# Two images' patches per block of partitions in the tokenizer's last layer and norm

## The chip, the cores and the metric

The kernel runs on one core of a Trainium2 chip. The metric is the device time of one launch in microseconds, from the core's first instruction to its last with what the launch itself adds. Engines are named as in the profile: PE (TensorE, matmuls), DVE (VectorE), ACT (ScalarE), POOL (GpSimd), SP (here only a queue that issues DMAs).

## The reference, cut to what matters

A tokenizer turns 32 images into 49 patch tokens of 192 features each, ends in a depthwise and a pointwise convolution and a layer norm over the features, and is followed by a state space block (Mamba) and an attention and mixture-of-experts block. Only the end of the tokenizer and how it meets the Mamba block matter here.

```
h = relu(dwconv(h, f1_dw, f1_pw, f1_pwb))
h = relu(dwconv(h, f2_dw, f2_pw, f2_pwb))
h = dwconv(loc + h, f3_dw, f3_pw, f3_pwb)          # [B, 192, 7, 7]
t = transpose(h.reshape(B, 192, 49), (0, 2, 1))     # [B, 49, 192]
mu = mean(t, -1); var = mean((t - mu) ** 2, -1)
t = (t - mu) / sqrt(var + 1e-05) * ln_g + ln_b
h = concatenate([cls, t, txt], axis=1)              # [B, 82, 192]
h = h + mamba(layernorm(h)); h = h + attention_and_experts(layernorm(h))
```

## The kernel before

The 32 images run in four chunks `c` of eight (`CH = 4`, `IM = 8`) through a pipeline of seven waves `w`. In wave `w`, chunk `w` is in the first convolutions, and the three fusion layers `f1`, `f2`, `f3` (index `k` = 0, 1, 2) work on chunks `w-1`, `w-2`, `w-3`. A depthwise layer has 192 channels in two tiles of 96 partitions: DVE does tile 0 with nine instructions of 441 elements that add up in PSUM (`dw`, lines 176 and 178), and ACT and POOL do tile 1 (nine products, `weigh`, L346; eight sums, `add_up`, L494). PE then does the pointwise layer. For `f1` and `f2` the result has channels in partitions (L239). For `f3` PE takes the image as the stationary operand, so that patches come out in partitions: each image gives 49 partitions x 192 (L302). Two images fill one PSUM bank, a *fill*; three banks rotate, so fill `n` waits until DVE has taken fill `n - 3`.

DVE takes a fill with the bias added (`take_rows`, L416) into `T0`, 49 partitions x 32 images x 192, computes mean and variance of each image's 49 rows (L422, L425), POOL computes the reciprocal root (`roots`, L481, L483, ready as `s_rs`), and `norm_rows` ends the norm: one instruction per image for `(t - mean) * root` (L431), then two over the whole chunk for `* ln_g` (L434) and `+ ln_b` (L436). SP stores each finished chunk into `H` (tokens in partitions) with one DMA (L206).

The order on each engine is the order in which the code is written. In wave `w` DVE runs `norm_rows(w-5)` and `take_rows(w-4)` ahead of the depthwise work of `f2` and `f3`; after the last wave it runs `take_rows(3)`, `norm_rows(2)`, `norm_rows(3)`. The Mamba block's first round is woven in through `tail(...)` points: `z` (L1182) from PE matmuls (L866, L869) and ACT (L1008 to L1047), which need the stored chunk 0; `R` (L1187) behind PE's L891; a zeroing of PSUM (L1271); then the statistics of the stored chunks 1 to 3 (`chunk_stats`, L1166 to L1173), the step size (L1190 to L1200), and the scan, whose inputs POOL makes (L1356) and which DVE runs (L1238).

Of the kernel before, what the change touches and what calls it, by code (L numbers as in the profile page):

```python
# [95 lines left out]
def tokenizer(nc, ctx, at, ps, H, vec, ident, eye, xcol, w_pl, w_pg, had, pw_mix, w96, vecs, pwb_row, lng_row, lnb_row, cls_row, txt):  # L96


    if True:
# [27 lines left out]
        T0 = P1[0:PATCHES].rearrange("p k n -> p (k n)")[:, 0:B * D].rearrange("p (b c) -> p b c", b=B)  # L127
        rows = sb("rows", [PATCHES, 3, D])
        st = sb("st", [PATCHES, IM, 6])
        mv = sb("mv", [PATCHES, B, 2])  # L130
        ve = sb("ve", [PATCHES, B])
        rs = sb("rs", [PATCHES, B])
        nh = sb("nh", [PATCHES, B])
# [3 lines left out]
        f3_bank = [psC[0:PATCHES, 0, 0:2 * D], psC[0:PATCHES, 1, 0:2 * D], psC[0:PATCHES, 2, 0:2 * D]]  # L137
# [52 lines left out]
        def sync(sp, tail):  # L190
# [13 lines left out]
            for c in range(CH):  # L204
                sp.wait_ge(s_t1, c + 1)
                sp.dma_start(H[1:1 + PATCHES, c * IM:(c + 1) * IM, :], T0[:, c * IM:(c + 1) * IM, :]).then_inc(s_out[c], 16)  # L206
                if c == 1:
                    sp.wait_ge(s_lr, CH)
                    tail("last sums")

        def tensor(pe, tail):
# [32 lines left out]
            for w in range(WAVES):  # L244
# [46 lines left out]
                if 0 <= w - 3 < CH:  # L291
# [5 lines left out]
                    for n in range(c * IM // 2, (c + 1) * IM // 2):  # L297
                        if n >= 3:
                            pe.wait_ge(s_t0, n - 2)
                        for j in range(2):  # L300
                            for k in range(2):
                                mm = pe.matmul(f3_bank[n % 3][:, j * D:(j + 1) * D], dense(DF[2], k)[:, 2 * n + j - c * IM, :],  # L302
                                               wf[:, 3, k, :], start=k == 0, stop=k == 1)
                        mm.then_inc(s_f[2], 1)

        def scalar(act, tail):
# [2161 lines left out]
```

## Time and profile before

| | |
|---|---|
| median of 3 runs | 1454.99 us (1440.70, 1454.99, 1455.33) |
| the profiled execution | 1444.48 us |
| its span, first to last instruction | 1442.7 us, 1.78 us less than its time |
| granted TensorE clock, mean over the span | 0.92 of full speed |
| busy share of the span | PE 85%, PEld 54%, DVE 72%, ACT 49%, POOL 54% |
| end of the tokenizer (first input of the scan starts on POOL) | 301.46 us after the start |

The busy shares are means over stages of different kinds. The change lies in the last 110 us of the first 301 us; what happens behind 301 us is the same program in both kernels, and starts when the step `dtz` of L1200 is done. A granted clock of 0.50 is the lower of TensorE's two levels (1.2 GHz), 1.00 the upper (2.4 GHz).

### The profile page before, as it was taken

How to read it: one execution, taken by the hardware profiler on the slowest of the kernel's cores; microseconds unless marked ns; L12 is line 12 of the kernel's file. 1: busy time of each engine (PE TensorE's matmuls, PEld its weight loads, DVE VectorE, ACT ScalarE, POOL GpSimd, SP SyncE). 2: the span in 40 equal slices, each digit the busy share in tenths (PEclk: the TensorE clock that was granted, in tenths of full speed). 3: DMA queues.
4: the chain of work that ended last, by engine and by line, in shares of the span. 5: the costliest groups of instructions: out<-in, count | busy, mean ns of one | idle time of the engine just before them, and what ended most of it. 6: DMA issues, size and time to landing. Idle time of an engine off the chain costs nothing.

```text
span 1442.7 us, 19486 instructions
## 1 busy us (share of the span) xinstructions
PE 1220.1 (85%) x5820; PEld 783.0 (54%) x5821; DVE 1043.2 (72%) x1983; ACT 705.7 (49%) x1490; POOL 778.8 (54%) x499
## 2 busy tenths in 40 slices
PE   6895845547889899999986789999999799999996
PEld 4342322223445445454543457887777567777775
DVE  3699778798989999999999745677778653333332
ACT  1137732167677686867675235545543232222221
POOL 3027975197787968788787420134445465222222
PEclk9797656779999999999999989999999599999998
DMA  5200000044042240404050001112222123222221
GB/s 171 57 1 0 29 9 29 17 162 141 12 130 70 72 140 0 140 0 140 11 160 1 0 5 57 42 47 72 56 64 65 36 54 54 38 37 35 37 36 20
DMA packets 71201, 81.00 MB, mean 56 GB/s; under 512 B 13230, under 2 KB 62917, under 8 KB 71129
## 3 DMA queue, kind: packets, MB, share of 16 engines
q1 hardware_dynamic: 51986, 69.29, 15.4%
q0 software_dynamic: 17152, 9.24, 4.7%
q10 hardware_dynamic: 1992, 1.59, 0.4%
q8 instruction: 37, 0.61, 0.2%
q14 instruction: 34, 0.28, 0.1%
HBM read 48.74 MB, written 30.01 MB: 55 GB/s over the span
## 4 chain that ended last, share of the span: by engine, by line
PE 55%; DVE 20%; ACT 9%; issue 8%; POOL 5%; DMA 2%; DVEq 0%; SPq 0%; POOLq 0%; ACTq 0%
PE ps L2131 10%; PE ps L955 6%; PE ps L2150 6%; DVE hs L1238 5%; PE ps L1610 3%; PE ps L866 3%; PE ps L1553 3%; POOL DF L494 2%; PE ps L239 2%; PE ps L2140 2%; PE ps L1623 2%; ACT ps L1108 2%; DVE ps L178 2%; PE ps L932 2%; PE ps L232 2%
## 5 line engine op out<-in xcount | busy, mean ns | idle before, releaser
L1356 POOL TENSOR_TENSOR Bx<-dtz,Bb 128x984 f32<-128x984 f32 x128 | 289.4, 2283 | 41.2 <-DVE hs L1238 27.3
L1238 DVE TENSOR_TENSOR_SCAN hs<-ps,Bx 128x492 f32<-128x492 f32 x256 | 287.6, 1164 | 22.2 <-POOL Bx L1356 12.8
L1108 ACT ACTIVATE ps<-dt,A 128x324 f32<-128x324 f32 (+1 forms) x512 | 211.5, 456 | 79.5 <-DVE hs L1238 76.5
L955 PE MATMUL ps<-hs,b_id 128*128 128x492 f32 x512 | 235.9, 583 | 12.0 <-DVE y L1205 9.3
L2250 POOL DMA_INDIRECT out<-yt,dest x48 | 74.7, 1557 | 166.4 <-DVE yt L2236 160.2
L1248 DVE TENSOR_TENSOR hs<-hs,ps 128x984 f32<-128x984 f32 x128 | 150.2, 1173 | 1.9
L2131 PE MATMUL ps<-W,xT 97*128 (+1 forms) x384 | 143.1, 516 | 3.8 <-ACT hb L2188 1.4
L955 PEld LDWEIGHTS ps<-hs,b_id 128*128 128x128 f32 x512 | 92.2, 193 | 79.1 <-issue 73.8
L2220 DVE COPY hT__5873<-ps 128x768 f32<-128x768 f32 x48 | 46.0, 958 | 115.8 <-PE ps L2140 113.6
L1999 POOL DMA_INDIRECT buckets<-XS,c_slot x64 | 90.9, 1420 | 38.2 <-issue 25.0
L2150 PE MATMUL ps<-W,hT__5873 128*128 x576 | 109.2, 327 | 0.8 <-DVE yb L2230 0.8
L2188 ACT ACTIVATE hb<-ps 128x768 f32<-128x768 f32 x48 | 39.0, 812 | 143.4 <-PE ps L2131 143.4
L2006 POOL TENSOR_TENSOR c_x<-c_x,bro 82x192 f32<-82x192 f32 x32 | 19.2, 600 | 161.7 <-DVE c_x L1795 161.6
L2131 PEld LDWEIGHTS ps<-W,xT 97*128 97x128 f32 (+1 forms) x384 | 71.8, 197 | 58.1 <-issue 21.6
L2150 PEld LDWEIGHTS ps<-W,hT__5873 128*128 128x128 f32 x576 | 91.4, 190 | 1.4 <-issue 1.4
L494 POOL TENSOR_TENSOR DF<-DF,prod 96x441 f32<-96x441 f32 x84 | 87.4, 1041 | 6.6
L940 PE MATMUL ps<-P,sel 96*128 96x328 bf16 x128 | 40.2, 315 | 52.8 <-DVE hs L1248 40.4
L1756 DVE TENSOR_REDUCE mx<-ps 82x12 f32<-82x984 f32 x32 | 37.6, 1176 | 60.4 <-PE ps L1610 60.4
L1623 PEld LDWEIGHTS ps<-V,PT 82*82 82x82 f32 x768 | 64.6, 160 | 10.8 <-issue 4.3
L940 PEld LDWEIGHTS ps<-P,sel 96*128 96x128 bf16 x128 | 12.3, 97 | 100.5 <-DVE hs L1248 65.9
L1623 PE MATMUL ps<-V,PT 82*82 82x17 f32 x768 | 63.1, 228 | 1.7 <-DVE XN L1788 1.7
L1610 PE MATMUL ps<-kB,qT 128*82 128x328 f32 (+1 forms) x256 | 61.9, 386 | 3.1 <-DVE E L1760 2.0
(273 smaller groups left out, 2424.4 us busy)
## 6 DMA issues: line engine op xcount, KB each, us to landing
Bb<-b_rows SPq DMA_DIRECT2D x32, 656.0 KB, 7.4
buckets<-b_zero SPq DMA_DIRECT2D x8, 2288.0 KB, 15.3
xg<-buckets SPq DMA_DIRECT2D x48, 104.0 KB, 2.0
xc<-in_xcol SPq DMA_DIRECT2D x4, 1176.0 KB, 9.3
W<-in_w1d SPq DMA_DIRECT2D x8, 582.0 KB
W<-in_w2d SPq DMA_DIRECT2D x8, 576.0 KB
out<-H SPq DMA_DIRECT2D x8, 246.0 KB
H<-P SPq DMA_DIRECT2D x4, 294.0 KB
```

The source lines that it names most:

```text
L494: g.tensor_tensor(out, a, prod[:, (9 * n + t) % PRODUCTS], ALU.add).then_inc(s_sum, 1)
L955: mm = pe.matmul(ps[:, BANK_Y + h, 0:HALF], ident[:], f2(hs[:, s % LONG])[:, h * HALF:(h + 1) * HALF], start=s == 0, stop=s == STATE - 1)
L1108: a = act.activation(ps[:, BANK_A + h, c:c + w].rearrange("p (g t) -> p g t", t=S)[:, :, 1:S], dt[:, (par + t // STATE) % 2, m, g0 * S:g1 ...
L1238: v.tensor_tensor_scan(f2(hs[:, t % LONG])[:, c], ps[:, BANK_A + h, 0:HALF], f2(Bx[:, t % RING])[:, c], 0.0, ALU.mult, ALU.add).then_inc(s ...
L1248: v.tensor_tensor(hs[:, s % LONG], hs[:, s % LONG], ps[:, BANK_C + s % 2, 0:N].rearrange("p (a n) -> p a n", a=1).broadcast_to([128, NI, N ...
L1356: g.tensor_tensor(Bx[:, t % RING], dtz[:, p], Bb[:, p, t % STATE, :].rearrange("p (a n) -> p a n", a=1).broadcast_to([128, NI, N]), ALU.mu ...
L1610: mm = pe.matmul(ps[0:S, SCORES + h0 // 6, (h0 % 6) * S:(h0 % 6 + h1 - h0) * S], qT[:, par, m_, q * S:(q + 1) * S], kB[:, par, m_, q, j:j ...
L1623: mm = pe.matmul(ps[0:S, HEAD_OUT + c % 2, h * (DH + 1):(h + 1) * (DH + 1)], PT[:, c % 2, h, :], V[:, vpar, c, h, :], start=True, stop=True)
L1999: g.indirect_dma_start(out=xs, out_offset=bass.IndirectOffsetOnAxis(ap=slot[:, p % 2, k, c:c + 1], axis=0), in_=slots(p)[:, c, :], in_offs ...
L2131: mm = pe.matmul(ps[:, UP + h, 0:384], xT[c_, p, k, :], W1[c_, k, bass.ds(e, 1), h * 384:(h + 1) * 384].rearrange("p a n -> p (a n)"), sta ...
L2150: mm = pe.matmul(ps[:, Y, 0:D], hT[:, p, k, :], W2[:, k, bass.ds(e, 1), :].rearrange("p a n -> p (a n)"), start=k == 0, stop=k == KF - 1)
L2250: g.indirect_dma_start(out=out, out_offset=bass.IndirectOffsetOnAxis(ap=dest[:, p:p + 1], axis=0), in_=yt[:, p, :], in_offset=None, comput ...
```

## The change

- The stationary operand of `f3` becomes two images at once. Images lie 56 columns apart in `DF` (eight rows of seven, the eighth row is padding), so 56 + 49 = 105 columns hold two images, and PE writes 105 partitions: image `2i` in partitions 0 to 48, image `2i+1` in 56 to 104, unused rows between. A chunk has four such pairs and two fills instead of eight images and four fills.
- `T0`, the rows of bias, scale and shift, and the statistics are laid out for 105 partitions and half as many blocks.
- `take_rows` now also does `(t - mean) * ln_g` in one fused instruction per pair; it needs no root. `norm_rows` is one fused instruction per pair, `t * root + ln_b`. Both have two tensor inputs in SBUF.
- `norm_rows(2)` moves ahead of `take_rows(3)`.
- Each chunk is stored by two DMAs of 49 partitions x 4 images x 192 instead of one of 49 x 1536.

```diff
+        TWO, PAIRS = ROW * GRID + PATCHES, IM // 2
+        T0 = P1[0:TWO].rearrange("p k n -> p (k n)")[:, 0:CH * PAIRS * D].rearrange("p (b c) -> p b c", b=CH * PAIRS)
...
-                sp.dma_start(H[1:1 + PATCHES, c * IM:(c + 1) * IM, :], T0[:, c * IM:(c + 1) * IM, :]).then_inc(s_out[c], 16)
+                images = H[1:1 + PATCHES, c * IM:(c + 1) * IM, :].rearrange("p (n h) d -> p h n d", h=2)
+                for h in range(2):
+                    sp.dma_start(images[:, h], T0[h * ROW * GRID:h * ROW * GRID + PATCHES, c * PAIRS:(c + 1) * PAIRS, :]).then_inc(s_out[c], 16)
...
-                    for n in range(c * IM // 2, (c + 1) * IM // 2):
+                    for n in range(c * FILLS, (c + 1) * FILLS):
                         if n >= 3:
                             pe.wait_ge(s_t0, n - 2)
                         for j in range(2):
+                            b = 4 * n + 2 * j - c * IM
                             for k in range(2):
-                                mm = pe.matmul(f3_bank[n % 3][:, j * D:(j + 1) * D], dense(DF[2], k)[:, 2 * n + j - c * IM, :],
+                                both = DF[2][:, k].rearrange("p r c -> p (r c)")[:, b * ROW * GRID:b * ROW * GRID + TWO]
+                                mm = pe.matmul(f3_bank[n % 3][:, j * D:(j + 1) * D], both,
                                                wf[:, 3, k, :], start=k == 0, stop=k == 1)
...
-                v.wait_ge(s_t0, (c + 1) * IM // 2)
-                for b in range(c * IM, (c + 1) * IM):
-                    i = own.did(v.bn_stats(st[:, b % IM, :], T0[:, b, :]))
+                v.wait_ge(s_t0, (c + 1) * FILLS)
+                for b in range(c * PAIRS, (c + 1) * PAIRS):
+                    i = own.did(v.bn_stats(st[:, b % PAIRS, :], T0[:, b, :]))
                 own.need(i)
-                for b in range(c * IM, (c + 1) * IM):
-                    v.bn_aggr(mv[:, b, :], st[:, b % IM, :]).then_inc(s_mv, 1)
+                for b in range(c * PAIRS, (c + 1) * PAIRS):
+                    v.bn_aggr(mv[:, b, :], st[:, b % PAIRS, :]).then_inc(s_mv, 1)
+                v.wait_ge(s_mv, (c + 1) * PAIRS)
+                for b in range(c * PAIRS, (c + 1) * PAIRS):
+                    i = own.did(v.scalar_tensor_tensor(T0[:, b, :], T0[:, b, :], mv[:, b, 0:1], rows[:, 1, :], ALU.subtract, ALU.mult))
+                own.need(i)
 
             def norm_rows(c):
 
                 v.wait_ge(s_rs, c + 1)
-                for b in range(c * IM, (c + 1) * IM):
-                    i = own.did(v.tensor_scalar(T0[:, b, :], T0[:, b, :], mv[:, b, 0:1], rs[:, b:b + 1], ALU.subtract, ALU.mult))
-                own.need(i)
-                t = T0[:, c * IM:(c + 1) * IM, :]
-                i = own.did(v.tensor_tensor(t, t, rows[:, 1:2, :].broadcast_to([PATCHES, IM, D]), ALU.mult))
-                own.need(i)
-                v.tensor_tensor(t, t, rows[:, 2:3, :].broadcast_to([PATCHES, IM, D]), ALU.add).then_inc(s_t1, 1)
+                for b in range(c * PAIRS, (c + 1) * PAIRS):
+                    i = v.scalar_tensor_tensor(T0[:, b, :], T0[:, b, :], rs[:, b:b + 1], rows[:, 2, :], ALU.mult, ALU.add)
+                i.then_inc(s_t1, 1)
...
+            norm_rows(CH - 2)
             take_rows(CH - 1)
-            norm_rows(CH - 2)
             tail("last rows")
             norm_rows(CH - 1)
```

On DVE in wave 5, from the norm of chunk 0 to the start of `f2`'s depthwise work of chunk 3, there stood before (`P_58` is `T0`, `mv` holds mean and variance, `rs` the root, `rows` bias, scale and shift):

```order
L431 TENSOR_SCALAR P_58<-P_58,mv,rs 49x192 x8
L434 TENSOR_TENSOR P_58<-P_58,rows 49x1536
L436 TENSOR_TENSOR P_58<-P_58,rows 49x1536
L416 TENSOR_TENSOR P_58<-ps,rows 49x384 x4
L422 BN_STATS st<-P_58 49x6 x8
L425 BN_AGGR mv<-st 49x2 x8
L176 TENSOR_SCALAR ps<-PF_60,vec 96x441
```

and now:

```order
L441 SCALAR_TENSOR_TENSOR P_58<-P_58,rs,rows 105x192 x4
L422 TENSOR_TENSOR P_58<-ps,rows 105x384 x2
L428 BN_STATS st<-P_58 105x6 x4
L431 BN_AGGR mv<-st 105x2 x4
L434 SCALAR_TENSOR_TENSOR P_58<-P_58,mv,rows 105x192 x4
L178 TENSOR_SCALAR ps<-PF_60,vec 96x441
```

The norm of chunk 0 is four instructions instead of ten, and four of another kind stand behind the statistics of chunk 1; the same two rows repeat in the other waves.

On DVE behind the last depthwise work (`DF_65` is its result) there stood before:

```order
L178 SCALAR_TENSOR_TENSOR DF_65<-PF_61,vec,ps 96x441
L416 TENSOR_TENSOR P_58<-ps,rows 49x384 x4
L422 BN_STATS st<-P_58 49x6 x8
L425 BN_AGGR mv<-st 49x2 x8
L431 TENSOR_SCALAR P_58<-P_58,mv,rs 49x192 x8
L434 TENSOR_TENSOR P_58<-P_58,rows 49x1536
L436 TENSOR_TENSOR P_58<-P_58,rows 49x1536
L1271 MEMSET ps 128x1024
L1182 SCALAR_TENSOR_TENSOR z<-sg,ps 128x328
```

and now:

```order
L180 SCALAR_TENSOR_TENSOR DF_65<-PF_61,vec,ps 96x441
L441 SCALAR_TENSOR_TENSOR P_58<-P_58,rs,rows 105x192 x4
L422 TENSOR_TENSOR P_58<-ps,rows 105x384 x2
L428 BN_STATS st<-P_58 105x6 x4
L431 BN_AGGR mv<-st 105x2 x4
L434 SCALAR_TENSOR_TENSOR P_58<-P_58,mv,rows 105x192 x4
L1277 MEMSET ps 128x1024
L1188 SCALAR_TENSOR_TENSOR z<-sg,ps 128x328
```

The norm of chunk 2 now stands ahead of the taking of chunk 3's fills, where DVE waits for PE.

On PE at the join of the two blocks, from the fills of chunk 2 over the Mamba block's first transposes (L860) and projections there stood before:

```order
L239 MATMUL ps<-DF_64,wf 96x392 x4
L302 MATMUL ps<-wf,DF_65 49x192 x16
L860 MATMUL ps<-b_id,hn 128x82 x8
L866 MATMUL ps<-hT,wzg 128x328 x2
L869 MATMUL ps<-hT,wzg 128x328 x2
```

and now:

```order
L243 MATMUL ps<-DF_64,wf 96x392 x4
L308 MATMUL ps<-wf,DF_65 105x192 x8
L866 MATMUL ps<-b_id,hn 128x82 x8
L872 MATMUL ps<-hT,wzg 128x328 x2
L875 MATMUL ps<-hT,wzg 128x328 x2
```

Eight matmuls of the same length replace sixteen (each stands as two records in the trace).

## Rows read from the trace of the kernel before

**Rows 1.** The chain that ended last, 190 to 262 us: start, length (us), what.

```profile
195.28 1.69 POOL rs L483
196.99 9.51 DVE P L431 x8
206.53 2.66 DVE P L434
...
211.48 2.81 PE ps L302 x8
...
235.95 8.42 PE ps L302 x32
...
259.36 8.67 PE ps L302 x32
```

**Rows 2.** Timeline of DVE: start, us, engine, line, operation, count, [idle before, releaser].

```profile
214.90 2.17 DVE L422 BATCH_NORM_STATS2 st<-P 49x6 f32<-49x192 f32 x8
217.10 0.63 DVE L425 BATCH_NORM_AGGREGATE mv<-st 49x2 f32<-49x6 f32 x8
...
235.99 2.40 DVE L431 TENSOR_SCALAR P<-P,mv,rs 49x192 f32<-49x192 f32 x8 [0.16 <-DVE DF L178]
...
240.21 1.75 DVE L436 TENSOR_TENSOR P<-P,rows 49x1536 f32<-49x1536 f32 x1
...
249.28 0.50 DVE L1182 SCALAR_TENSOR_TENSOR z<-sg,ps 128x328 f32<-128x328 f32 x1 [4.33 <-ACT sg L1047]
...
252.47 0.50 DVE L1182 SCALAR_TENSOR_TENSOR z<-sg,ps 128x328 f32<-128x328 f32 x1
...
268.05 0.55 DVE L416 TENSOR_TENSOR P<-ps,rows 49x384 f32<-49x384 f32 x1 [0.75 <-PE ps L302]
...
277.53 0.91 DVE L1271 MEMSET ps<- 128x1024 f32 x1 [0.21 <-issue]
278.36 0.47 DVE L1182 SCALAR_TENSOR_TENSOR z<-sg,ps 128x328 f32<-128x328 f32 x1
...
284.64 0.48 DVE L1187 TENSOR_TENSOR R<-ps,P 64x328 f32<-64x328 f32 x1
...
291.85 2.17 DVE L1166 BATCH_NORM_STATS2 b_st<-H 82x6 f32<-82x192 f32 x8
...
299.65 1.67 DVE L1200 TENSOR_TENSOR dtz<-dt,z 128x984 f32<-128x984 f32 x1
```

**Rows 3.** Timeline of POOL.

```profile
196.94 1.98 POOL L520 TENSOR_TENSOR PF<-L,R 96x392 f32<-96x392 f32 x2
...
199.94 7.62 POOL L494 TENSOR_TENSOR DF<-DF,prod 96x441 f32<-96x441 f32 x7
...
253.55 1.66 POOL L483 TENSOR_TENSOR rs<-ve,nh 49x8 f32<-49x8 f32 x1
```

**Rows 4.** Groups of DVE by form: busy us, mean ns of one.

```profile
L1205 DVE SCALAR_TENSOR_TENSOR y<-z,vec,ps 128x164 f32<-128x164 f32 x16 | 5.4, 376 | 0.0
```

**Rows 5.** Timeline of ACT.

```profile
237.25 5.08 ACT L346 ACTIVATE prod<-PF,vec 96x441 f32<-96x441 f32 x9
244.84 0.54 ACT L1008 ACTIVATE hT<-ps,vec 128x328 f32<-128x328 f32 x1 [2.52 <-PE ps L860]
```

**Rows 6.** Timeline of PE.

```profile
246.62 1.34 PE L866 MATMUL ps<-hT,wzg 128*128 128x328 f32 x4 [1.53 <-ACT hT L1011]
247.89 0.82 PE L869 MATMUL ps<-hT,wzg 64*128 64x328 f32 x4
...
278.98 5.54 PE L891 MATMUL ps<-z,wx 128*96 128x328 f32 x12 [8.92 <-DVE z L1182]
```

**Rows 7.** Windows: stretch, length, busy us (count) of PE, PEld, DVE, ACT, POOL, granted clock, DMA share, GB/s.

```profile
50.00:54.00 4.00, 3.40 (x5) 1.03 (x6) 0.39 (x1) 0.00 (x0) 0.00 (x0) 0.62 1.09 277
240.00:242.00 2.00, 2.00 (x8) 1.25 (x7) 1.97 (x3) 2.00 (x5) 0.00 (x0) 0.50 0.00 0
242.00:244.00 2.00, 2.00 (x13) 1.51 (x12) 1.44 (x3) 0.32 (x1) 0.00 (x0) 0.97 0.20 52
```

More of the change, by code:

```diff
@@ L125, in tokenizer @@
         R2 = sb("R2", [HD, 2, NP])
[L127 to L133, printed above, removed]
+        TWO, PAIRS = ROW * GRID + PATCHES, IM // 2
+        T0 = P1[0:TWO].rearrange("p k n -> p (k n)")[:, 0:CH * PAIRS * D].rearrange("p (b c) -> p b c", b=CH * PAIRS)
+        rows = sb("rows", [TWO, 3, D])
+        st = sb("st", [TWO, PAIRS, 6])
+        mv = sb("mv", [TWO, CH * PAIRS, 2])
+        ve = sb("ve", [TWO, CH * PAIRS])
+        rs = sb("rs", [TWO, CH * PAIRS])
+        nh = sb("nh", [TWO, CH * PAIRS])
         psC, psF, psA, psB = ps[:, 0:3, :], ps[:, 3, :], ps[:, 4:6, :], ps[:, 6:8, :]
-        f3_bank = [psC[0:PATCHES, 0, 0:2 * D], psC[0:PATCHES, 1, 0:2 * D], psC[0:PATCHES, 2, 0:2 * D]]
+        f3_bank = [psC[0:TWO, 0, 0:2 * D], psC[0:TWO, 1, 0:2 * D], psC[0:TWO, 2, 0:2 * D]]
+        FILLS = PAIRS // 2
         s_wp = sem("a_wp"); s_small = sem("a_small"); s_wc = sem("a_wc"); s_x = [sem("a_x0"), sem("a_x1")]
@@ L311, in scalar @@
             for k, row in enumerate((pwb_row, lng_row, lnb_row)):
-                act.dma_start(rows[:, k, :], row.rearrange("(a c) -> a c", a=1).broadcast_to([PATCHES, D])).then_inc(s_rows, 16)
+                act.dma_start(rows[:, k, :], row.rearrange("(a c) -> a c", a=1).broadcast_to([TWO, D])).then_inc(s_rows, 16)
             act.wait_ge(s_small, 64)
@@ L412, in take_rows @@
             def take_rows(c):
-                for n in range(c * IM // 2, (c + 1) * IM // 2):
+                for n in range(c * FILLS, (c + 1) * FILLS):
                     v.wait_ge(s_f[2], n + 1)
                     v.tensor_tensor(T0[:, 2 * n:2 * n + 2, :], f3_bank[n % 3].rearrange("p (j c) -> p j c", j=2),
-                                    rows[:, 0:1, :].broadcast_to([PATCHES, 2, D]), ALU.add).then_inc(s_t0, 1)
+                                    rows[:, 0:1, :].broadcast_to([TWO, 2, D]), ALU.add).then_inc(s_t0, 1)
@@ L477, in roots @@
             def roots(c):
-                g.wait_ge(s_mv, (c + 1) * IM)
-                a = slice(c * IM, (c + 1) * IM)
+                g.wait_ge(s_mv, (c + 1) * PAIRS)
+                a = slice(c * PAIRS, (c + 1) * PAIRS)
                 n = own.did(g.tensor_scalar(ve[:, a], mv[:, a, 1], 1e-5, None, ALU.add))
@@ L505, in gpsimd @@
                         if w - k - 1 > 0:
[L506 removed]
+                            g.wait_ge(s_f[k], (w - k - 1) * (FILLS if k == 2 else 1))
                         add_up(k, w)
@@ L820, in _ @@
                 if j == 0:
-                    sp.wait_ge(tok.s_out[CH - 1], 16)
+                    sp.wait_ge(tok.s_out[CH - 1], 32)
                     sp.dma_start(wug[:], w_ug).then_inc(s_wug, 16)
@@ L943, in first @@
             def first():
-                pe.wait_ge(tok.s_t0, CH * IM // 2)
+                pe.wait_ge(tok.s_t0, CH * IM // 4)
                 pe.sem_inc(s_left, 1)
@@ L1163, in chunk_stats @@
                 a = slice(c * IM, (c + 1) * IM)
-                v.wait_ge(tok.s_out[c], 16)
+                v.wait_ge(tok.s_out[c], 32)
                 for b in range(c * IM, (c + 1) * IM):
@@ L1269, in tail @@
                 if point == "last rows":
-                    v.wait_ge(tok.s_t0, CH * IM // 2)
+                    v.wait_ge(tok.s_t0, CH * IM // 4)
                     v.memset(ps[:, BANK_A:BANK_A + 2, :], 0.0).then_inc(s_cst, 1)
```

3 lines of the change are left out of this document (1 added, 2 removed).

## Prediction

> **What bounds the kernel now.** I read the chain of waits first, from 190 to 302 us. From 195.28 us it runs over POOL's root, then DVE's norm of chunk 0, PE's fills and DVE's depthwise work, down to `dtz`, whose end starts the scan [rows 1, 2]. So DVE sets the end of the tokenizer, with PE in between twice: the fills of chunk 2 and of chunk 3, 8.42 and 8.67 us, each of which DVE needs whole before it goes on [rows 1]. Ahead of 195 us POOL's sums set the pace, and DVE waits for their root; what is saved on DVE there is worth nothing. Behind 301 us both kernels run the same program, begun by one event, so an earlier `dtz` shifts all of it. The second view is the timeline of POOL beside DVE's. The same eight norm instructions (L431) cost 9.51 us beside POOL's additions and 2.40 us when POOL is idle [rows 1, 2]; 1.98 us for POOL's pair L520 and seven times its pitch of 7.62 / 7 = 1.09 us make 9.6 [rows 3]. Each of them gets one gap between two POOL instructions. The addition of 1536 elements shows the same: 2.66 us with POOL at work, 1.75 us without [rows 1, 2]. Third, the granted clock: it is at the lower level when a group of fills begins and rose at about 242 us, six microseconds into the fills of chunk 2; in the two windows PE did 8 and then 13 matmul records in 2 us [rows 7].
>
> **The price of the new instruction.** No instruction of the trace adds two SBUF tensors with a scalar read per partition. The nearest (L1205, 164 elements, one input in PSUM) took 376 ns [rows 4]; with 28 elements more it is about 400 ns, or 0.37 us from start to start, so four cost 1.5 us when POOL is idle. Beside POOL's chain the bounds are those 0.37 us (no conflict) and 1.98 us each (each waits for a pair like L520). I take 1.09 us, the pitch at which L431 went, since the addition with two SBUF inputs was held up in the same way.
>
> The Trainium skill (SBUF — State Buffer, Who interferes with whom) says that DVE and GpSimd share a pair of ports by an exclusive lock, and that a DVE instruction with two SBUF inputs needs it against a GpSimd instruction that reads SBUF. It agrees with the 9.51 and 2.66 us. By it the four cost a POOL instruction each; without it they would cost 1.5 us together.
>
> **The change step by step**, each as how much earlier something ends than before.
>
> 1. Ahead of 195 us (taking chunk 0): four fused instructions more, about 4.4 us, against two fills and eight statistics less. DVE waits for POOL's root afterwards anyway. Nothing, as long as POOL itself isn't slowed (a rival below).
> 2. Norm of chunk 0: 9.51 + 2.66 + 1.75 = 13.9 us before [rows 1, 2], 1.98 + 3 x 1.09 = 5.3 us now, since POOL's L520 starts at the same moment [rows 3]. **8.6 us** gained (12.4 without conflict, 6.0 at 1.98 each).
> 3. Taking chunk 1: before from 210.9 to 217.7 us, with 2.81 us of PE on the chain because the fourth fill waits for a bank [rows 1, 2]. Now both fills are ready: 2 x 0.5 + 2.8 / 2 + 4 x 1.09 = 6.8 us. **Nothing** (+2.9 without conflict, -3.6 at 1.98). POOL no longer waits for the fourth fill before it adds up the next chunk, and stays busy to about 216 us; that is off the path.
> 4. Fills of chunk 2: 16 records for 32, 4.2 to 4.7 us for 8.42, about 4 gained at PE. But the projection behind them needs ACT for `hT`, and ACT is in its nine products, which ended at 237.25 + 5.08 = 242.3, only 2.5 us ahead of `hT` at 244.84 [rows 5]. These products move with step 2. So `hT` comes 8.6 + 2.5 = 11.1 us earlier, not 12.6. The norm of chunk 1 lies under PE's fills.
> 5. First `z`: PE's four and four records took 1.34 + 0.82 us at the upper clock [rows 6, 7]. The new stretch of PE is some 5.5 us with the transposes, so whether the clock is up by then is open. Upper: 11.1 stays. Lower: 2.2 us more, 8.9.
> 6. Second `z` (3.2 us after the first, rows 2): statistics 1.4 us, four fused instructions beside an addition and the root (1.66 us, rows 3) about 2.4, `z` 0.5: 4.3 us. **10.0** at the upper level. At the lower PE needs 4.3 us plus ACT and DVE 1.0: 5.3, which leaves 6.8.
> 7. Fills of chunk 3: 8.67 us of 32 records halve at the lower clock to about 4.6 [rows 1]. **4.1** more: 14.1, or 10.9. The norm of chunk 2 (1.5 us) now lies in this wait.
> 8. Last statistics and norm: 268.60 to 277.53 = 8.9 us before the zeroing [rows 2], now 1.4 + 2.4 = 3.8 (the four meet POOL's root again; 2.9 if they don't, 4.8 if all wait). **5.1** more: 19.2, or 16.0. PE's third projection fits beside it.
> 9. From the last `z` to `R` it was 5.8 us, the norm of chunk 3 [rows 2]. That norm is now 1.5 us, and `R` waits for the first half of L891, 2.8 to 3.7 us, and ACT's two readings of 0.4 each [rows 6]: 4.5 us. **1.3** more: 20.5, or 17.3.
> 10. From `R` to `dtz` DVE is busy throughout; the same.
>
> I take the middle of step 9, **19 us**, because the clock's rise falls just at the edge. On the profiled execution that gives 1444.5 - 19 = 1425.5 us. That execution was 10.5 us under the median of the three runs, which came at 1440.7 and twice at 1455; the four lie at two levels. On the median it would be 1436. I forecast 1431 us, between the two, and the range takes both in.
>
> The Trainium skill (TensorE: Matmul & The Clock Gate, HAM oscillation — how this bites in real kernels) says that idle gaps of PE drop its clock, so that short bursts start cold each time. It speaks against this change: half the matmuls, the same gaps. By it the lower figures of steps 5 to 9 hold, a gain of 17.3 us instead of 20.5; the row at 240 us agrees in kind.
>
> **Rivals.**
>
> - *No conflict with POOL.* If the fused instruction passes POOL's additions, steps 2 and 3 give 12.4 + 2.9 = 15.3 us; but then POOL's sums and root (to about 218 us) become the bound of ACT's products and `hT`, which gain about 12 + 2.5. With 0.9 us in step 8: 24.5 us, 1420 us on the profile's level. The 2.66 us speaks against it. 15%.
> - *POOL is held up in turn.* A fused instruction streams 192 elements one by one and may hold POOL for its own 0.34 us or so. Four lie ahead of 195 us, where POOL is the bound: 1.4 us; eight more reach POOL's root of chunk 1 and through L520 `hT`: some 1.6 us. Gain 16, 1428.5 us. Against it: POOL's pitch beside the eight L431 was no longer than usual, 7.62 us for seven [rows 3]. The same page on SBUF gives this rule, that whoever comes first holds the pair for its whole instruction. 15%.
> - *Heavy conflict.* Every fused instruction waits 2 us: steps 2 and 3 give 6.0 - 3.6 = 2.4 us instead of 8.6, steps 6 and 8 lose 1 or 2 more. Gain about 11, 1433.5 us, within 1%. 12%.
> - *The stores come late (slower than before).* The two stores of chunk 3 move pieces of 768 bytes instead of 6 KB. Chunk 3's statistics (291.85 before, rows 2) now come 10.4 us after the issue. From there on every microsecond of landing counts; to be slower than before by 1% they must land some 10 + 19 + 14 = 43 us after the issue. The text tokens, pieces of the same 768 bytes, flowed at 277 GB/s [rows 7], so 0.3 MB takes about 1 us and a few of latency. 2%.
>
> **How the numbers follow.** Forecast (17 to 21 us gained) 52%, the rivals as above, 4% for what I don't see. The measurement of this kernel tells about 1% from no change, 14.5 us. Faster by more than that: the forecast, the first two rivals, less some for the two levels of the runs, 0.78. Within 1%: heavy conflict and runs that fall on different levels, 0.19. Slower by over 1%: 0.03. The range goes from 1440.7 - 24 = 1417 to 1455.3 - 10 = 1445.
>
> **What would show it.** In the changed kernel's timeline: the four fused instructions at 197 us take about 5.3 us and the four behind chunk 1's statistics 4.4 (1.5 each if there is no conflict); `f2`'s last depthwise work starts at about 209 us instead of 217.7; the fills of chunk 2 last 4.2 to 4.7 us; `z` waits for ACT behind its products; `R` waits for PE; the first scan input at about 282.5 us instead of 301.46. From there to the end both traces should be equally long. I am wrong if POOL's additions come at a pitch well over 1.1 us, if the statistics of chunk 3 wait for a DMA, or if the part behind the first scan input has another length.

## The result and the profile after

| | before | changed kernel |
|---|---|---|
| median of the timed runs | 1447.85 us (1438.40, 1440.70, 1454.99, 1455.33) | 1426.89 us (1422.24, 1424.70, 1429.09, 1430.85) |
| ratio, 95% interval | | 0.985 (0.9809 to 0.9891) |
| profiled execution, its span | 1444.48, 1442.7 us | 1429.09, 1427.3 us |
| first input of the scan on POOL | 301.46 us | 282.70 us |
| from there to the last instruction | 1141.2 us | 1144.6 us |
| mean granted clock | 0.920 | 0.917 |

The changed kernel is faster by 1.5%, and the interval excludes 1.0: it reaches from 1.1 to 1.9%. Ratios here and below leave out single executions that were slowed as a whole (in one kernel below an execution took 1544 us, at a mean granted clock of 0.79). 1426.89 us lies 4 us from the forecast of 1431, inside the range of 1417 to 1445. The first input of the scan came at 282.70 us, forecast at 282.5. What the span lost (15.4 us) is less than that gain (18.8 us), because the same program behind it took 3.4 us more in this execution; further down that part differs by more than this between executions of equal code.

The chain that ended last, changed kernel: start, length, what.

```profile
196.47 1.06 POOL rs L489
197.55 4.35 DVE P L441 x4
...
205.24 3.34 DVE P L434 x3
...
228.56 4.98 ACT prod L352 x9
...
252.02 5.46 PE ps L308 x16
...
262.83 2.23 PE ps L897 x6
```

Beside [rows 1] two things have changed. The norm of chunk 0 is one row of 4.35 us where rows of 9.51 and 2.66 us stood, and behind them one of 1.75 us, at 209.21. The fills of chunk 2 have left the chain: ACT's nine products stand in their place, and PE's fills end under them. The fills of chunk 3 are still on it.

DVE's timeline, to be laid beside [rows 2] (the bracket is the idle time ahead and who ended it):

```profile
197.55 4.35 DVE L441 SCALAR_TENSOR_TENSOR P<-P,rs,rows 105x192 f32<-105x192 f32 x4 [5.54 <-POOL rs L489]
201.82 1.01 DVE L422 TENSOR_TENSOR P<-ps,rows 105x384 f32<-105x384 f32 x2
...
204.45 4.12 DVE L434 SCALAR_TENSOR_TENSOR P<-P,mv,rows 105x192 f32<-105x192 f32 x4
208.71 0.68 DVE L178 TENSOR_SCALAR ps<-PF,vec 96x441 f32<-96x441 f32 x1
...
227.08 1.40 DVE L441 SCALAR_TENSOR_TENSOR P<-P,rs,rows 105x192 f32<-105x192 f32 x4 [0.15 <-DVE DF L180]
...
240.06 0.50 DVE L1188 SCALAR_TENSOR_TENSOR z<-sg,ps 128x328 f32<-128x328 f32 x1 [6.98 <-ACT sg L1053]
...
245.13 0.49 DVE L1188 SCALAR_TENSOR_TENSOR z<-sg,ps 128x328 f32<-128x328 f32 x1 [1.67 <-ACT sg L1053]
...
257.51 0.56 DVE L422 TENSOR_TENSOR P<-ps,rows 105x384 f32<-105x384 f32 x1 [2.00 <-PE ps L308]
...
259.69 1.41 DVE L434 SCALAR_TENSOR_TENSOR P<-P,mv,rows 105x192 f32<-105x192 f32 x4
261.38 0.91 DVE L1277 MEMSET ps<- 128x1024 f32 x1 [0.29 <-DVE P L434]
...
265.88 0.49 DVE L1193 TENSOR_TENSOR R<-ps,P 64x328 f32<-64x328 f32 x1 [1.88 <-ACT P L1058]
...
266.38 2.16 DVE L1172 BATCH_NORM_STATS2 b_st<-H 82x6 f32<-82x192 f32 x8
```

The same kind of fused instruction costs two different times here: four at 197.55 and four at 204.45 us took 4.35 and 4.12 us, four at 227.08 us took 1.40 us. POOL's timeline tells what lay beside them:

```profile
197.50 2.10 POOL L526 TENSOR_TENSOR PF<-L,R 96x392 f32<-96x392 f32 x2
...
200.72 7.64 POOL L500 TENSOR_TENSOR DF<-DF,prod 96x441 f32<-96x441 f32 x7
...
226.44 0.22 POOL L1322 TENSOR_TENSOR b_nb<-b_root,b_negm 82x16 f32<-82x16 f32 x1
232.56 0.96 POOL L500 TENSOR_TENSOR DF<-prod 96x441 f32<-96x441 f32 x1 [5.91 <-PE ps L308]
```

POOL adds without a pause beside the first eight, and stands idle from 226.7 us, beside the fast four. Its seven additions took 7.64 us and its pair 2.10, as against 7.62 and 1.98 in [rows 3]: the fused instructions waited, POOL hardly did. ACT and PE answer to [rows 5] and [rows 6]:

```profile
228.46 5.08 ACT L352 ACTIVATE prod<-PF,vec 96x441 f32<-96x441 f32 x9
233.45 0.51 ACT L1014 ACTIVATE hT<-ps,vec 128x328 f32<-128x328 f32 x1
```

```profile
227.03 5.45 PE L308 MATMUL ps<-wf,DF 96*105 96x192 f32 x16 [6.68 <-DVEq L184]
...
235.20 2.53 PE L872 MATMUL ps<-hT,wzg 128*128 128x328 f32 x4 [1.63 <-ACT hT L1017]
...
240.60 2.56 PE L872 MATMUL ps<-hT,wzg 128*128 128x328 f32 x4 [1.48 <-DVE z L1188]
...
252.02 5.45 PE L308 MATMUL ps<-wf,DF 96*105 96x192 f32 x16 [7.46 <-DVEq L184]
257.26 1.33 PE L872 MATMUL ps<-hT,wzg 128*128 128x328 f32 x4
```

The same four records of L872 took 2.53 and 2.56 us, then 1.33. The windows of the changed kernel, read as [rows 7], show why:

```profile
234.00:236.00 2.00, 0.80 (x2) 0.62 (x3) 0.00 (x0) 1.05 (x2) 1.84 (x3) 0.50 0.26 100
240.00:242.00 2.00, 1.40 (x3) 0.98 (x4) 1.91 (x9) 0.00 (x0) 1.31 (x2) 0.50 0.01 4
256.00:258.00 2.00, 2.00 (x8) 1.77 (x7) 0.49 (x1) 0.00 (x0) 0.00 (x0) 0.66 0.31 91
258.00:260.00 2.00, 1.34 (x7) 0.37 (x5) 1.90 (x10) 0.44 (x1) 0.26 (x1) 1.00 0.00 0
264.00:266.00 2.00, 2.00 (x6) 1.04 (x5) 0.12 (x1) 0.76 (x2) 0.00 (x0) 0.55 0.13 33
```

In [rows 7] the clock had risen by 242 us, within a group of 32 records. Now it is still at 0.50 behind the 16 records and the eight transposes; the first two projections both go at the lower level, and it rises only at the very end of the fills of chunk 3 (0.66 in the window at 256 us, 1.00 in the next). The window at 264 us lies in the last projection.

### The profile page after: what moved, and what is told of

Same layout as the page of the kernel before. It is cut to its first block, busy times and chain, and to the rows that moved or that the text cites. A ratio compares the mean times of both kernels' runs of the same rounds, so it can differ in the third digit from the quotient of the medians.

```text
span 1427.3 us, 19317 instructions
## 1 busy us (share of the span) xinstructions
PE 1210.3 (85%) x5756; PEld 783.2 (55%) x5757; DVE 1022.4 (72%) x1935; ACT 705.8 (49%) x1490; POOL 777.2 (54%) x499
## 4 chain that ended last, share of the span: by engine, by line
PE 52%; DVE 23%; issue 8%; ACT 8%; POOL 5%; DMA 3%; DVEq 0%; SPq 0%; POOLq 0%; ACTq 0%
PE ps L2137 10%; PE ps L2156 6%; PE ps L961 6%; DVE hs L1244 6%; DVE ps L180 5%; PE ps L1616 3%; PE ps L1559 3%; PE ps L872 3%; PE ps L2146 2%; ACT ps L1114 2%; PE ps L1629 2%; PE ps L938 2%; PE ps L897 2%; PE ps L915 2%; PE ps L875 2%
## 5 line engine op out<-in xcount | busy, mean ns | idle before, releaser
L2256 POOL DMA_INDIRECT out<-yt,dest x48 | 74.8, 1558 | 164.7 <-DVE yt L2242 156.3
```

What stands on the lines that cost most here:

```text
L2256: g.indirect_dma_start(out=out, out_offset=bass.IndirectOffsetOnAxis(ap=dest[:, p:p + 1], axis=0), in_=yt[:, p, :], in_offset=None, comput ...
```

## The experiments

How they are compared: the whole time of one kernel differs between its executions by more than the effects asked for (the kernel before ran in 1438.05 to 1461.57 us in one series). So each profile is read over one *stretch*: from the end of POOL's root of chunk 0 (before 196.95, changed kernel 197.52 us) to the start of the scan's first input on POOL. It was 104.5 us before and 85.2 us in the changed kernel. Ratios are to the kernel before, run beside it on the same chip. The times of the medians come from several chips and are compared only by these ratios, but for the second reordering, beside which the changed kernel was run again.

| kernel | root's end, first input, us | stretch, us | median, us | ratio (95%) |
|---|---|---|---|---|
| before | 196.95, 301.46 | 104.5 | 1447.85 | |
| changed | 197.52, 282.70 | 85.2 | 1426.89 | 0.985 (0.9809 to 0.9891) |
| changed, unaltered, again | 197.15, 282.14 | 85.0 | 1429.15 | 0.9851 (0.9803 to 0.9899) |
| pairs only | 199.15, 286.24 | 87.1 | 1438.48 | 0.9929 (0.9888 to 0.9969) |
| fused steps only | 197.68, 304.70 | 107.0 | 1453.07 | 1.0049 (1.0012 to 1.0085) |
| changed, norm of chunk 2 in its old place | 197.26, 284.61 | 87.3 | 1430.64 | 0.9877 (0.982 to 0.9934) |
| changed, first fused step of chunk 1 late | 200.79, 281.58 | 80.8 | 1429.86 | 0.9866 (0.9808 to 0.9924) |
| changed, both `z` late | 196.94, 279.48 | 82.5 | 1426.54 | 0.987 (0.978 to 0.9959) |
| changed, idle matmuls | 196.33, 279.76 | 83.4 | 1432.51 | 0.9885 (0.9843 to 0.9926) |
| first reordering | 199.05, 279.70 | 80.7 | 1428.26 | 0.9833 (0.9746 to 0.9921) |
| first reordering, idle matmuls | 200.05, 280.68 | 80.6 | 1423.65 | 0.9845 (0.9754 to 0.9937) |
| second reordering | 200.11, 274.94 | 74.8 | 1418.75 | 0.9787 (0.974 to 0.9833) |
| second reordering, idle matmuls | 196.99, 271.12 | 74.1 | 1422.98 | 0.979 (0.9745 to 0.9835) |

The theories at the start: **A**, the pairs carry the gain, with half the instructions beside POOL's additions and half the fills, and fusing pays back beside POOL what it saves; **B**, the fused norm carries a good part of it. The first three experiments divide the change.

By their timed runs, none of the single moves that follow these three, nor either kernel of the first reordering, can be told from the changed kernel: the intervals overlap. What is said of them rests on the stretch of one profiled execution each; the changed kernel's, taken twice, was 85.2 and 85.0 us.

**Pairs only.** Two images per block as in the change, but the norm in its three old steps and in its old place:

```diff
-                v.wait_ge(s_mv, (c + 1) * PAIRS)
-                for b in range(c * PAIRS, (c + 1) * PAIRS):
-                    i = own.did(v.scalar_tensor_tensor(T0[:, b, :], T0[:, b, :], mv[:, b, 0:1], rows[:, 1, :], ALU.subtract, ALU.mult))
-                own.need(i)
...
-                    i = v.scalar_tensor_tensor(T0[:, b, :], T0[:, b, :], rs[:, b:b + 1], rows[:, 2, :], ALU.mult, ALU.add)
-                i.then_inc(s_t1, 1)
+                    i = own.did(v.tensor_scalar(T0[:, b, :], T0[:, b, :], mv[:, b, 0:1], rs[:, b:b + 1], ALU.subtract, ALU.mult))
+                own.need(i)
+                t = T0[:, c * PAIRS:(c + 1) * PAIRS, :]
+                i = own.did(v.tensor_tensor(t, t, rows[:, 1:2, :].broadcast_to([TWO, PAIRS, D]), ALU.mult))
+                own.need(i)
+                v.tensor_tensor(t, t, rows[:, 2:3, :].broadcast_to([TWO, PAIRS, D]), ALU.add).then_inc(s_t1, 1)
...
+            take_rows(CH - 1)
             norm_rows(CH - 2)
-            take_rows(CH - 1)
```

> Two images per block of partitions, but the old norm (subtract and scale per block, then two additions and multiplications over the chunk) and the old order at the end. Measured at the first scan input (301.46 us before, 282.70 after the whole change). Theory A (the pairs carry the gain, the fusion pays back beside POOL what it saves): the norm of chunk 0 takes 4 x 1.07 + 2 x (0.9 to 1.6), about 7.0 us instead of 4.35, but taking chunk 1 only 2.6 us instead of 6.7, so the first scan input comes at about 282.5 us, as with the whole change. Theory B (the fused norm that does not wait carries a good part): the norm steps left as they were cost at least the 5 us that chunk 0 alone gained, 287 us or later.

Measured, on DVE:

```profile
199.18 4.05 DVE L437 TENSOR_SCALAR P<-P,mv,rs 105x192 f32<-105x192 f32 x4 [10.01 <-POOL rs L489]
203.26 1.70 DVE L440 TENSOR_TENSOR P<-P,rows 105x768 f32<-105x768 f32 x1
205.00 1.75 DVE L442 TENSOR_TENSOR P<-P,rows 105x768 f32<-105x768 f32 x1
206.68 1.01 DVE L422 TENSOR_TENSOR P<-ps,rows 105x384 f32<-105x384 f32 x2
```

The three steps take 7.5 us for a chunk, where the fused one takes 4.35; but the fused kernel pays 4.12 us right behind it, for the first steps of chunk 1. Counted from the root's end, the last taps of `f2` (its nine depthwise instructions on DVE, for chunk 3) start after 10.0 us here and after 11.2 in the changed kernel. The stretch is 87.1 us: 17.4 of the 19.3 us come from the pairs alone. By the time of the first input, 286.24 us, the run lies nearer to B's 287 us than to A's 282.5. But 1.6 us of the miss lie ahead of the stretch, and neither number had counted the old order, which the third experiment prices at 2.2 us: 85.0 and 2.2 make 87.2 us for A, measured 87.1. By its timed runs the kernel gave about half of the gain, and its interval just meets that of the changed kernel. The granted clock goes with that difference: the executions at a mean clock of 0.915 to 0.918 took 1425.2 to 1431.4 us, in the changed kernel 1424.1 to 1430.2, and the slower five went at 0.906 to 0.909. Whether the order of this kernel brings the lower clock on is not shown.

**Fused steps only.** 49 partitions, eight images a chunk, four fills, one store, with the two fused steps:

```diff
-        TWO, PAIRS = ROW * GRID + PATCHES, IM // 2
+        T0 = P1[0:PATCHES].rearrange("p k n -> p (k n)")[:, 0:B * D].rearrange("p (b c) -> p b c", b=B)
...
-                for b in range(c * PAIRS, (c + 1) * PAIRS):
+                for b in range(c * IM, (c + 1) * IM):
```

> One image per block as before, but the norm in the two fused steps; old order at the end. Theory A: eight fused instructions of 1.07 us behind POOL's additions in the norm of chunk 0 (8.6 instead of 13.9 us), and eight more behind chunk 1's statistics (8.6 us more), then 2.4 us more between the first and second z, against 2.6 us gained before R: the first scan input at about 304 us, 2 to 4 us later than before. Theory B: some 5 to 9 us earlier than before, 293 to 296 us.

```profile
198.38 8.16 DVE L435 SCALAR_TENSOR_TENSOR P<-P,rs,rows 49x192 f32<-49x192 f32 x8 [0.15 <-DVE DF L178]
...
213.35 6.61 DVE L428 SCALAR_TENSOR_TENSOR P<-P,mv,rows 49x192 f32<-49x192 f32 x8
```

Together 14.8 us, where the old norm had 13.9. With one image per block fusing raises the number of instructions per chunk from 10 to 16, and most of them lie beside POOL's additions: the stretch is 107.0 us, 2.5 more than before, and the ratio is above 1. B is refuted, and A's forecast (304 us) met by 304.70.

**The norm of chunk 2 in its old place.**

```diff
-            norm_rows(CH - 2)
             take_rows(CH - 1)
+            norm_rows(CH - 2)
```

> The whole change except that the norm of chunk 2 stands behind the taking of chunk 3 again. Theory A: its 1.4 us leave PE's shadow and stand on the path: first scan input at 284.1 us instead of 282.7. Rival: the reordering hides more than itself, since the old place also met POOL's root: 285.5 us or later.

The stretch was 87.3 us, 2.2 more. The norm itself is 1.4 of that; `R` waited 2.81 us instead of 1.88:

```profile
267.78 0.49 DVE L1193 TENSOR_TENSOR R<-ps,P 64x328 f32<-64x328 f32 x1 [2.81 <-ACT P L1058]
```

The last projection began 1.0 us later than in the changed kernel and met the lower clock sooner, from about 264.2 us on, half a microsecond behind its start. Set beside pairs only (87.1), this kernel, pairs and fused steps in the old order, shows that fusing gained nothing in the paired layout either, where it raises the count from 6 to 8.

**First fused step of chunk 1 late.** It moves from ahead of `f2`'s taps to right in front of the second step, one wave later:

```diff
+                if c != 1:
+                    centre(c)
...
+                if c == 1:
+                    centre(c)
```

> The whole change, but the first fused step of chunk 1 (subtract, scale) is done in wave 6 right ahead of the second, where POOL is idle and DVE waits for PE's fills, instead of beside POOL's additions in wave 5. It tells the price of the conflict: the four instructions took 4.12 us there. Theory A (they wait for POOL's instructions): they take 1.4 us in the new place and nothing on the path; the last depthwise work of f2 starts 4.1 us earlier, POOL's root of chunk 1 then becomes the bound, and the first scan input comes about 2.9 us earlier, at 279.8 us. Rival (on 105 partitions they are that slow by themselves): 4 us in either place, no gain or a loss.

```profile
227.93 1.40 DVE L421 SCALAR_TENSOR_TENSOR P<-P,mv,rows 105x192 f32<-105x192 f32 x4 [0.15 <-DVE DF L180]
```

The same four instructions took 1.40 us instead of 4.12, because POOL was idle there. The stretch fell by 4.4 us to 80.8, and the rival, that the instruction is that slow by itself on 105 partitions, is excluded. The forecast had 2.9; the rest came with the clock, at whose upper level the second projection ran this time (1.37 us, 2.56 in the changed kernel).

**Both `z` late.** They stand behind the last taps, so that DVE does not wait for ACT in front of them:

```diff
-                if w == WAVES - 1:
-                    tail("last taps")
...
+                if w == WAVES - 1:
+                    tail("last wave")
+                    tail("last taps")
```

> The whole change, but the two first z of the Mamba block stand behind the last depthwise work of f3 on DVE instead of around the statistics ahead of it. After the change DVE waits 6.98 us for the first z, then 1.67 us for the second, and only then starts that work. Theory A (this wait is on the path and is what the change ran into): the depthwise work starts some 9 us earlier, the second z and PE's order then bound chunk 3's fills, which start at about 247 instead of 252 us: 4 to 5 us earlier, 80.5 us behind the root. Rival (PE's projections are the bound anyway): no change, as the fills stand behind the second z's matmuls in PE's order.

```profile
234.14 4.68 DVE L432 SCALAR_TENSOR_TENSOR P<-P,mv,rows 105x192 f32<-105x192 f32 x4
...
250.60 0.50 DVE L1187 SCALAR_TENSOR_TENSOR z<-sg,ps 128x328 f32<-128x328 f32 x1 [4.51 <-ACT sg L1052]
```

2.6 us, not 4 to 5: the wait for the first `z` (6.98 us) went, but the fused steps of chunk 2 moved under POOL's additions (4.68 us for 1.41), and the second `z` waits for ACT in its turn.

**Idle matmuls.** Nine matmuls whose results nobody reads ahead of the fills of chunk 2, nine ahead of those of chunk 3:

```diff
+                if w == WAVES - 2:
+                    pe.wait_ge(s_r1, CH)
+                    for q in range(9):
+                        pe.matmul(psB[0:HD, 1, 0:NP], wf[:, 1, 0, 0:HD], dense(DF[0], 0), start=True, stop=True)
...
+                    pe.wait_ge(s_r2, CH)
+                    for q in range(9):
+                        pe.matmul(psA[0:HD, 1, 0:NP], wf[:, 1, 0, 0:HD], dense(DF[0], 0), start=True, stop=True)
```

> The whole change, with nine matmuls whose result nobody reads ahead of the fills of chunk 2 (PE is idle there for 6.7 us) and nine ahead of those of chunk 3 (7.5 us idle). Measured from POOL's root of chunk 0 to the first scan input (85.15 us after the change, 104.47 before), since what lies ahead of the root varies by up to 4 us. Theory A (halving the fills left PE at the lower clock, which costs the change 2 us at each of the first two z and 2.8 us at chunk 3's fills): with the clock held up, the fills take about 2.7 us instead of 5.45, the four and four records of the first z 2.2 instead of 4.0, and the first scan input comes 5 to 6 us earlier, 79 to 80 us behind the root. Rival (the chain is DVE's and ACT's and the clock hardly matters): at most 1 us earlier.

```profile
225.88 2.85 PE L315 MATMUL ps<-wf,DF 96*105 96x192 f32 x16 [1.05 <-DVEq L184]
...
233.74 2.53 PE L879 MATMUL ps<-hT,wzg 128*128 128x328 f32 x4 [4.45 <-ACT hT L1024]
...
250.56 2.85 PE L315 MATMUL ps<-wf,DF 96*105 96x192 f32 x16 [0.22 <-DVEq L184]
```

Both groups of fills took 2.85 us instead of 5.45. Of these 5.2 us only 1.8 reached the end, nearer to the rival's 1 us than to A's 5 to 6. Behind the fills of chunk 2 PE waited 4.45 us for `hT`, since ACT ends its products no sooner, and was back at the lower level for the projections; `R` waited 3.00 us, with the last projection partly at the lower level.

**First reordering.** Besides the two moves above, the taps of `f2` for chunk 3 stand ahead of the norm of chunk 0, and ACT's nine products ahead of its four rows `hn`, which normalise chunk 0 for the Mamba block. The second kernel adds idle matmuls as above.

> The whole change with four orders changed: the first fused step of chunk 1 in wave 6, in wave 5 the last depthwise work of f2 ahead of the norm of chunk 0 and the taking of chunk 1 (DVE waits 5.5 us for the root there), the two z behind the last depthwise work, and ACT's nine last products ahead of its four normalised rows. Theory A, by the steps as read from the trace after: first z at 38 us behind the root instead of 43, fills of chunk 3 at 42.5 instead of 54.5, first scan input at 74 us instead of 85.15. Rival (POOL's sums and root become the bound right away): no more than the 4.4 us that the deferred step alone gave, 80.8 us.

> The same with idle matmuls that hold the clock up: four ahead of chunk 2's fills and six behind them. Theory A: the two first z cost 1.8 us less each and the fills of chunk 3 up to 2.8 less, first scan input at 69 us behind the root. Rival (clock without weight): 74 us, as without them.

```profile
211.84 2.17 DVE L1180 BATCH_NORM_STATS2 b_st<-H 82x6 f32<-82x192 f32 x8 [2.70 <-DMA H<-P]
...
233.49 4.68 DVE L421 SCALAR_TENSOR_TENSOR P<-P,mv,rows 105x192 f32<-105x192 f32 x4
```

80.7 us, the rival's number. The norm of chunk 0 is stored later, so its statistics (`chunk_stats`) now wait for the DMA; and the fused steps of chunk 2 meet POOL. With idle matmuls it was 80.6 us, but these did not do what they were put in for:

```profile
226.94 5.30 PE L315 MATMUL ps<-wf,DF 96*105 96x192 f32 x16 [8.65 <-DVEq L184]
...
250.36 5.45 PE L315 MATMUL ps<-wf,DF 96*105 96x192 f32 x16
```

Both groups of fills went at the lower level all the same, PE having waited 8.65 us behind the idle matmuls for the first. So this kernel tells nothing of what a higher clock would be worth in this order.

**Second reordering.** It mends both: a group of taps stands between the store and the statistics, and the first fused step of chunk 2 too waits for the second. The first `z` stands behind the statistics of chunk 2 and ahead of the last taps, the second behind them.

```diff
-                v.wait_ge(s_mv, (c + 1) * PAIRS)
-                for b in range(c * PAIRS, (c + 1) * PAIRS):
-                    i = own.did(v.scalar_tensor_tensor(T0[:, b, :], T0[:, b, :], mv[:, b, 0:1], rows[:, 1, :], ALU.subtract, ALU.mult))
-                own.need(i)
+                if c not in (1, 2):
+                    centre(c)
+                if c == CH - 2:
+                    tail("last wave")
...
+                if c in (1, 2):
+                    centre(c)
...
                 if w == WAVES - 2:
-                    tail("last but one taps")
+                    norm_rows(w - 5)
+                    take_rows(w - 4)
                 if 0 <= w - 3 < CH:
...
+                if w == WAVES - 2:
+                    tail("last but one taps")
+                if w == WAVES - 1:
+                    tail("last taps")
```

> The changed kernel with VectorE's rows between POOL's root of chunk 0 and the first scan input reordered: the first fused steps of chunks 1 and 2 move from ahead of the root to right in front of their second steps; the depthwise taps that feed chunk 3 stand ahead of the norm of chunk 0; the z rows stand behind the last taps and the statistics of chunk 2; on ScalarE the last nine products stand ahead of the copies that depend on the norms. Stretch from the end of POOL's root of chunk 0 to the first scan input: 85.2 us in the changed kernel, 80.65 with the earlier reordering. Theory A (VectorE's own row sets the end; what it still waits for are the fills and projections that this order starts earlier): 75 us, so about 10 less than the changed kernel, some 1417 us. Rival B (POOL's sums and roots of chunks 1 to 3 set the end, or the fused steps run beside POOL's sums at four times their time): 80 us or more, no better than the earlier reordering.

> The same order, with idle matmuls on TensorE ahead of the fills of chunk 2 (6), behind them (9) and ahead of the fills of chunk 3 (6), so that it does not stand idle there. Theory A (the fills and the projections behind them run at the lower clock in this stretch and are waited for): the fills take 2.85 us instead of 5.45 and the projections 1.37 instead of 2.53, and the stretch is 3 to 4 us shorter than without them, 71 to 72 us. Rival B (the waits left are VectorE's and POOL's own): no shorter than without them, within 1 us.

> The changed kernel itself, unaltered, so that it stands in the same call as the two reorderings. Stretch from POOL's root of chunk 0 to the first scan input 85 us, within 1; median within 1% of 1427 us. What lies ahead of that root may differ by up to 4 us from run to run, as it did so far; if it differs here, that part is no effect of any order.

DVE's timeline in the second reordering:

```profile
203.62 4.04 DVE L447 SCALAR_TENSOR_TENSOR P<-P,rs,rows 105x192 f32<-105x192 f32 x4 [0.15 <-DVE DF L180]
...
216.66 2.17 DVE L1181 BATCH_NORM_STATS2 b_st<-H 82x6 f32<-82x192 f32 x8 [0.23 <-DVE DF L180]
...
238.05 0.50 DVE L1197 SCALAR_TENSOR_TENSOR z<-sg,ps 128x328 f32<-128x328 f32 x1 [9.27 <-ACT sg L1062]
...
245.47 1.40 DVE L421 SCALAR_TENSOR_TENSOR P<-P,mv,rows 105x192 f32<-105x192 f32 x4
...
258.11 0.49 DVE L1202 TENSOR_TENSOR R<-ps,P 64x328 f32<-64x328 f32 x1 [2.12 <-ACT P L1067]
```

The wait of 5.54 us for POOL's root has gone (0.15 us, and that is for DVE's own result), the statistics do not wait for the DMA, and chunk 2's first steps cost 1.40 us. The stretch is 74.8 us, 10.2 shorter than that of the changed kernel on the same chip (85.0); the medians of six runs each differ by as much, 1418.75 and 1429.15 us, and the highest run of the one (1426.78) lies under the median of the other. Their intervals, 0.974 to 0.9833 and 0.9803 to 0.9899, still overlap by a little.

A's number came (75 us), but not all of its reason. DVE's own row does not set the end of this stretch: it stands idle for 9.27 us ahead of the first `z`. The chain that ended last runs on POOL up to 223.95 us (additions, root, the pair L535), then over ACT's nine products and `hn`, PE and ACT to that `z`. That is the bound that rival B named, only lower than it was priced.

The idle matmuls gave 0.7 us more, no more than the rival's number, since the same POOL and ACT rows stand ahead of the first `z` there: the fills took 2.76 and 2.85 us, but the last projection fell back to the lower level and `R` waited 3.18 us instead of 2.12.

## Why the prediction was right

The forecast of 1431 us held, and its sum, 19 us earlier at the first input of the scan, was 18.8. Point by point:

- **Step 1.** The four more fused instructions ahead of the root took 4.39 us, and DVE then waited 5.54 us for the root. The root's end moved by 0.6 us (196.95 to 197.52), less than between variants whose code ahead of it is equal, where it lay from 196.3 (idle matmuls) to 200.8 us (first fused step of chunk 1 late). As forecast.
- **Step 2.** 13.9 us became 4.3, so 9.6 gained for 8.6. The step charged the first instruction the whole of POOL's pair, 1.98 us; each of the four went at about POOL's pitch.
- **Step 3.** Taking chunk 1 took 6.9 us, forecast 6.8. The pairs-only kernel shows what this nothing is made of: two fills and half the statistics less (2.5 us instead of 6.8), and the 4.1 of the fused steps more.
- **Step 4.** `hT` came 11.4 us earlier (233.45 for 244.84), forecast 11.1, and by the mechanism named: it follows ACT's products without a wait. But the fills took 5.45 us and not 4.2 to 4.7. That was just hidden: PE's transposes behind them ended at 233.6 us, when the products did.
- **Steps 5 and 6.** The lower branch held: 9.2 and 7.3 us for 8.9 and 6.8. The clock stayed at the lower level through both.
- **Step 7.** 3.2 us for 4.1: the mis-sized term. The step halved 8.67 us as if all 32 records had run at the lower clock. They had not: 16 records take 5.45 us at the lower level and 2.85 at the upper, and the clock of the kernel before rose at 266.0 us, so the last 2.0 us of these fills, about a third of the records, ran at the upper one:

```profile
264.00:266.00 2.00, 2.00 (x8) 1.32 (x7) 0.55 (x1) 0.00 (x0) 0.00 (x0) 0.50 0.00 0
266.00:268.00 2.00, 2.00 (x13) 1.30 (x11) 0.55 (x1) 0.00 (x0) 0.00 (x0) 1.00 0.00 0
```

  Halving took that cheap part away first, and what is left runs at the lower level. The last fill was taken 10.5 us earlier, not 10.9.
- **Step 8.** 5.6 for 5.1: the four fused instructions beside the root took 1.41 us, not 2.4. POOL's root ran from 260.28 to 261.33 us, beside them, and cost them nothing. The zeroing started 16.15 us earlier, forecast 16.0.
- **Step 9.** 2.6 for 1.3, the largest miss: the norm of chunk 3 is no longer on the path, as forecast, but the first half of the last projection took 2.23 us and not 2.8 to 3.7. It began at the upper clock, which fell to 0.50 at about 264.2 us, 1.4 us in, and `R` waited only 1.88 us.
- **Step 10.** From `R` to the first input 16.8 us in both.

The path and its waits were right; that the sum hit to 0.2 us was luck. The 19 us were the middle of two branches, and no mechanism gives a middle. What held is the lower branch, 17.3 us, and the misses within it (0.5 us more over the two `z`, 0.9 less in step 7, 0.5 and 1.3 more in steps 8 and 9) add up to the rest. The 1431 us are partly luck as well: they lie between the level of the profiled execution and the median of three runs, 1454.99 us, and the median before came out at 1447.85 with four. On the profile's own level the forecast was 1425.5 us and the execution took 1429.09.

Of the signs that were to show the forecast wrong, one came up: the part behind the first scan input has another length, 3.4 us more. The last section tells what goes with such differences. Fusing, which the steps did not price apart, was in sum worth nothing: with it and without it the stretch is 87.3 and 87.1 us.

Of the rivals, *no conflict* and *heavy conflict* are excluded by the 4.35 and 4.12 us, one POOL instruction each. (The 24.5 us of the first can't be had from its own terms, which give 23.3 to 24.8.) *POOL held up in turn* did not happen beside the fused steps (7.64 us for seven). *The stores come late* did not: the statistics at 266.38 us follow `R` without a wait. That the short bursts of PE start at the lower clock, which the prediction took from the Trainium skill (TensorE: Matmul & The Clock Gate, HAM oscillation — how this bites in real kernels), agrees with the trace: 0.50 at both groups of fills and both first projections. The last projection does not fit it: behind 3.49 us of idle time it began at 1.00 and fell to 0.50 while PE was at work. And of the two rows laid beside the rule on two SBUF inputs, only the 2.66 us belongs to an instruction with two such tensors; L431, with 9.51 us, reads one.

## What to carry to other kernels

Short DVE instructions on SBUF cost about one POOL instruction each while POOL adds beside them (four took 4.35 us, eight 8.16): halve their count, or move them to where POOL stands idle (4.12 us became 1.40), and give DVE independent work where it would wait for POOL's root. Fusing bought nothing here, because per chunk it left more instructions than it took away (16 for 10, or 8 for 6): count the instructions beside POOL, not the passes. When PE's work is halved, ask at which clock each part ran: here the part that went was the one at the upper clock. And a burst made faster is worth nothing if the next engine in the chain is already the one waited for.

## What was not expected of the hardware

- DVE can hold POOL up too. In the pairs-only kernel, beside the two long additions of 768 elements, POOL's seven additions took longer than in any other kernel here:

```profile
202.15 8.83 POOL L500 TENSOR_TENSOR DF<-DF,prod 96x441 f32<-96x441 f32 x7
...
220.06 2.00 POOL L489 TENSOR_TENSOR rs<-ve,nh 105x4 f32<-105x4 f32 x1
```

  8.83 us for 7.64, and a root of 2.00 us for 1.04, this one beside DVE's cast of `sel` (220.79 us, 1.22 long). In the changed kernel the root ended before the cast began and took 1.04. The root beside the cast took 1.99 us in the second reordering with idle matmuls as well. In the kernel with the first fused step of chunk 1 late it went the other way: the cast began beside POOL's additions and took 2.02 us, and POOL's 105x4 step behind them took 1.20 us instead of 0.23. This agrees with the rule of the Trainium skill (SBUF — State Buffer, Who interferes with whom) that the shared ports are an exclusive lock, whoever comes first; the fused instructions, 0.35 us each when POOL is idle, left next to no mark on POOL, and beside its root (step 8) neither side lost anything. The cause was read from these coincidences and not tried apart.
- Equal code does not take equal time. The part behind the first input of the scan is the same program in all these kernels, and took from 1137.2 us (both `z` late) to 1156.4 us (norm of chunk 2 in its old place) in the profiled executions; what lies ahead of the stretch differed by up to 4.5 us, as told at step 1. A difference of a few microseconds in this kernel is to be read between two events of the trace, and not from the span. The granted clock goes with these times. In the series on the chip of the second reordering the kernel before took 1438.05 us at a mean clock of 0.923 and 1456.49 us at 0.912. Of the two profiled executions just named the part behind the first input spent about 82 us at the lower level in the shorter and about 119 in the longer, an estimate from the mean clock of forty windows each; 19 us more time, 37 us more at half clock. Why the clock differs between executions of one kernel was not tried.
